# The b matrices of the next projection split behind the first softmax, and the coefficients evicted ahead of the second wide part

## The reference

```python
def cond(x, A, B, ids):
    Bx = jnp.einsum('bni,bri->bnr', x, B[ids])
    return jnp.einsum('bnr,bor->bno', Bx, A[ids])

def ffn(x, W, b, A, Bm, Wr):
    base_out = jnp.einsum('bsi,oi->bso', x, W) + b
    gates = jax.nn.softmax(jnp.einsum('bsi,ei->bse', x, Wr), axis=-1)
    lora_out = jnp.einsum('bser,eor->bseo', jnp.einsum('bsi,eri->bser', x, A), Bm)
    return base_out + jnp.einsum('bse,bseo->bso', gates * 2.0, lora_out)
```

## Time and profile before

| | before |
|---|---|
| median of three runs | 351.79 us (350.92 to 352.30) |
| the profiled execution, its own time | 353.02 us |
| its span, first to last instruction | 351.0 us |
| TensorE matmul busy | 326.0 us, 93% |
| VectorE busy | 246.0 us, 70% |
| ScalarE busy | 149.8 us, 43% |
| GpSimd busy | 89.9 us, 26% |
| mean granted TensorE clock | 0.976 of full |

### The profile page before, as it was taken

How to read it: one execution, slowest core, us unless ns; L and a number is a source line. 1 busy time by engine, 2 the same in 40 slices (tenths; PEclk the granted TensorE clock), 3 DMA queues, 4 the chain that set the end, 5 groups by cost and what they waited for, 6 DMA issues and landing times.

```text
span 351.0 us, 6577 instructions
## 1 busy us (share of the span) xinstructions
PE 326.0 (93%) x2112; PEld 304.6 (87%) x2112; DVE 246.0 (70%) x496; ACT 149.8 (43%) x317; POOL 89.9 (26%) x61
## 2 busy tenths in 40 slices
PE   6998747889999999999999999999999999999975
PEld 5777647879999899989999999999999999999864
DVE  5925993797586867697668767775878586855554
ACT  5856833663065405550456036613562166203210
POOL 0014620184015500550046003620262026300000
PEclk9999898969999999999999999999999999999989
DMA  6889526611782078405950586048803780140005
GB/s 276 327 278 326 181 92 203 219 58 51 250 269 92 17 228 287 132 2 166 302 189 0 143 289 225 0 120 268 266 5 98 245 296 18 49 190 2 0 23 218
DMA packets 31525, 56.17 MB, mean 160 GB/s; under 512 B 3793, under 2 KB 21074, under 8 KB 31506
## 3 DMA queue, kind: packets, MB, share of 16 engines
q1 hardware_dynamic: 31506, 55.94, 47.9%
HBM read 39.15 MB, written 16.78 MB: 159 GB/s over the span
## 4 chain that ended last, share of the span: by engine, by line
PE 53%; issue 12%; DMA 10%; DVE 9%; POOL 6%; SPq 5%; ACT 4%; POOLq 0%; ACTq 0%; DVEq 0%
PE ps_d L316 12%; PE ps_d L318 12%; PE ps_d L317 12%; POOL xs_lo L917 5%; DMA xraw<-w 4%; DMA out<-xraw 3%; PE ps_h L323 3%; PE ps_p L316 2%; DVE k_lo L684 2%; PE ps_p L317 2%; PE ps_p L318 2%; PE ps_t L447 2%; DMA abraw<-ab_tab 2%; SPq L233 2%; SPq L235 2%
## 5 line engine op out<-in xcount | busy, mean ns | idle before, releaser
L917 POOL TENSOR_TENSOR xs_lo<-xraw,xs_hi 128x512 fp32r<-128x512 f32 x48 | 67.8, 1423 | 195.4 <-ACT xs_hi L520 195.3
L316 PE MATMUL ps_d<-w1s_hi,a1s_hi 128*128 128x384 f32 (+1 forms) x216 | 72.7, 337 | 1.8 <-DVE w1s_lo L684 1.8
L318 PE MATMUL ps_d<-w1s_hi,a1s_lo 128*128 128x384 f32 (+1 forms) x216 | 70.2, 325 | 0.0
L317 PE MATMUL ps_d<-w1s_lo,a1s_hi 128*128 128x384 f32 (+1 forms) x216 | 70.2, 325 | 0.0
L903 DVE SCALAR_TENSOR_TENSOR xraw<-ps_d,bsum,xraw 128x512 f32<-128x512 f32 x62 | 46.3, 750 | 27.5 <-PE ps_d L318 27.5
L520 ACT ACTIVATE xs_hi<-xraw 128x512 fp32r<-128x512 f32 x64 | 38.4, 624 | 17.6 <-DMA xraw<-x_in 11.1
L316 PEld LDWEIGHTS ps_d<-w1s_hi,a1s_hi 128*128 128x128 f32 x216 | 41.1, 190 | 3.9 <-DVE w1s_lo L684 3.8
L316 PE MATMUL ps_p<-xs_hi,bst_hi 128*128 128x256 f32 x128 | 39.4, 307 | 3.4 <-POOL xs_lo L917 2.5
L317 PEld LDWEIGHTS ps_d<-w1s_lo,a1s_hi 128*128 128x128 f32 x216 | 41.1, 190 | 0.0
L318 PEld LDWEIGHTS ps_d<-w1s_hi,a1s_lo 128*128 128x128 f32 x216 | 41.0, 190 | 0.0
L317 PE MATMUL ps_p<-xs_lo,bst_hi 128*128 128x256 f32 x128 | 37.8, 295 | 0.0
(11 more groups left out here) (156 smaller groups left out, 691.8 us busy)
## 6 DMA issues: line engine op xcount, KB each, us to landing
xraw<-x_in SPq DMA_DIRECT2D x32, 512.0 KB, 5.0
out<-xraw SPq DMA_DIRECT2D x32, 512.0 KB, 3.6
xraw<-w SPq DMA_DIRECT2D x16, 512.0 KB, 6.5
abraw<-ab_tab SPq DMA_DIRECT2D x64, 128.0 KB, 2.1
b0raw<-b_tab SPq DMA_DIRECT2D x64, 64.0 KB, 1.9
b0raw<-a SPq DMA_DIRECT2D x1, 512.0 KB, 3.7
lp<-exp SPq DMA_DIRECT2D x4, 69.0 KB, 7.5
cm<-exp_in SPq DMA_DIRECT2D x1, 144.0 KB, 5.3
```

What stands on the lines that cost most here:

```text
L316: pe.matmul(acc, lh, rh, start=first, stop=False, skip_group_check=True)
L317: pe.matmul(acc, lh, rl, start=False, stop=False, skip_group_check=True)
L318: return pe.matmul(acc, ll, rh, start=False, stop=final, skip_group_check=True)
L917: return pool.tensor_tensor(dst, whole, high.bitcast(F32), ALU.subtract)
```

## The change

On ScalarE and VectorE, in steps 1 to 6, `split_b(g + 1)` moves from the head of the step to behind the first softmax, and `coef_high(0)` / `coef_low(0)` move ahead of `wide_high(1)` / `wide_low(1)`. Step 7 has no `split_b`; there only the coefficients change places with the wide part. Step 0 keeps its order. On TensorE the wait for `f1_lo` stands ahead of `start_results` in step 7, and where it was in the others.

```diff
@@ TensorE
                 if last:
+                    pe.wait_ge(f1_lo, 2 * g + 2)
                     start_results((0, 1, 3))
                 else:
                     project(g + 1, 0)
-                pe.wait_ge(f1_lo, 2 * g + 2)
+                    pe.wait_ge(f1_lo, 2 * g + 2)
                 route(1, k2, f1s)
@@ ScalarE
                 if not first:
                     h_and_k1(g)
-                if not last and not first:
-                    split_b(g + 1)
...
                 softmax_exp(0)
                 if first:
                     experts_high()
-                wide_high(1)
-                coef_high(0)
+                    wide_high(1)
+                    coef_high(0)
+                else:
+                    if not last:
+                        split_b(g + 1)
+                    coef_high(0)
+                    wide_high(1)
@@ VectorE
                 if not first:
                     h_to_sbuf(g)
                     k1_low(g)
-                if not last and not first:
-                    split_b(g + 1)
...
                 softmax(0)
                 if first:
                     experts_low()
-                wide_low(1)
-                coef_low(0)
+                    wide_low(1)
+                    coef_low(0)
+                else:
+                    if not last:
+                        split_b(g + 1)
+                    coef_low(0)
+                    wide_low(1)
```

## The result

The changed kernel takes 357.65 us (median of four runs, 356.15 to 359.33) against 351.60 for the kernel before: ratio 1.0163, interval 1.0106 to 1.0219. It is slower, by 6.0 us in these medians; the forecast was 355.9, the range 352.3 to 357.9.

What follows compares the result with a forecast made beforehand. TensorE was taken as the bound; five steps at 0.8 us (4.0) plus 0.1 for step 2 gave 4.1 us, on 351.8 a forecast of 355.9 us. The range meant to hold 8 in 10 was 352.3 to 357.9.

Steps and rivals of the forecast that it cites:

- The bound and the head of the step: TensorE bounds the loop; removing the b splits from the step's head, where they fill a gap, gains 0.
- ScalarE, VectorE, the coefficients: Behind the first softmax: coefficients reach TensorE 0.24 us later, costing 0.12 us, and everything that follows moves by 0.12.
- GpSimd's chunks and the reversal: Second half: GpSimd's chunks come late, GpSimd starts 0.18 us ahead of VectorE's `xs_lo`, and TensorE gets that chunk later.
- The price of a step: Steps 1, 3, 4, 5 and 6: 0.8 us each from the late chunk, 4.0 us together.
- Step 2 has its stall already: 0.1: Step 2 already had GpSimd ahead of VectorE at `xs_lo`, so the change adds only 0.1 us there.
- the forecast's own: The forecast's narrower range, 354.8 to 357.5 us, from 0.6 to 1.1 us in five steps.
- No reversal (1): VectorE stays ahead of GpSimd at `xs_lo`; a step costs 0.12 to 0.15 us, 351.8 to 352.5 us; chance 0.15.
- Rival 2: VectorE slower behind the softmax, coefficients 0.37 us late, VectorE stays first; about 2 us, 353.9 us; chance 0.08.
- Rival 4: Late `xs_lo` makes `turn()` wait too, or step 2 pays in full; 1.2 to 1.4 us a step; chance 0.07.

Runs made afterwards that it cites:

- the second measurement: The changed kernel again, unaltered, in more rounds against the kernel before: 358.58 us against 352.52, ratio 1.0149 (1.0101 to 1.0197).

## Why the prediction was right, and where its sizes were off

**The bound and the head of the step: right.** In steps 3 to 6 the exponential and `turn()` stand where they stood, to 0.01 us (step 2 is another matter, below). The b splits lay in a gap, and taking them out of it brought nothing.

**ScalarE, VectorE, the coefficients: right.** The weight load comes at 16.55 (forecast 16.53), and what follows moved by 0.14 (forecast 0.12): `ps_s` from 17.43 to 17.57. Where both kernels read `k_lo` from PSUM, the change costs 0.12 us a step, as this term alone would.

**GpSimd's chunks and the reversal: right, to 0.03 us in each line of the table.** The margin, forecast at 0.18, was 0.20. That the reversal is the larger part was tested from two sides: with the order held in both kernels 0.35 of the 0.85 remain, and with `k_lo` out of GpSimd's way in both kernels 0.12 remain. So of the 0.85 some 0.12 is the late coefficients, 0.23 that the first `k_lo<-cm` is held up longer (1.49 us, where it took 1.27), and 0.50 the reversal.

**The price of a step: 0.85 where 0.8 was said.** The same terms: the chunk reaches TensorE 0.73 later where 0.70 was said, the first matmul behind the wait costs its 0.10, and 0.02 more is added by the end of the step.

**Step 2: the term that was mis-sized.** "Step 2 has its stall already: 0.1" was wrong; it cost 0.44 (0.50 in the second execution of the changed kernel). The stall was indeed there already, but everything ahead of it moved by far more than the 0.12 of the other steps: VectorE's operation on `ps_s` went from 17.30 to 17.78 us into the step. In the kernel before, an x chunk landed late in step 2 (ScalarE waited 1.29 us for it). So GpSimd started its second chunk at 141.80, behind the softmax's subtraction on `lg` at 141.43, which took its 0.18 us; it held up only a later operation of the softmax, for less, and what follows came 0.13 us sooner than in step 4.

In this execution of the changed kernel the chunk was copied 0.5 us earlier in the step. GpSimd started at 142.16, ahead of the subtraction at 142.26, which took 1.22 us. The exponential moved from 11.19 to 12.23 us into the step, and what follows it came 0.21 later than in step 4. With the 0.14 of the other steps these two, 0.13 and 0.21, make up the 0.48. The second execution had a late chunk again, with the subtraction at 0.17 us, and its step 2 took 37.32 all the same. So the course of step 2 depends on when a chunk lands, which the prediction did not consider.

The sum is 4.7 us in the trace, not 4.1: 0.34 of the difference is step 2, the rest the five times 0.05.

**The rest, 351.6 + 4.7 = 356.3 against a median of 357.65.** Both intervals of the ratio hold 4.7 us. The median lies within the range (to 357.9) but just outside the forecast's own (to 357.5; its terms add up to 357.4). What the second measurement leaves above it (5.2) isn't explained by anything in the traces and may be the spread of single runs.

**The rivals.** No reversal (1) did not come true for the changed kernel, but did for the b splits alone, where all is 1.0 us late: there too it was no gain. Rival 2, slower operations on VectorE: the four `bst_lo` took 2.48 us (218.68 to 221.16), as worked out. The prediction says that the trace disagrees with the Trainium skill there; it doesn't, for the passage that it names (VectorE: DVE Perf Modes, The DRAIN you can't avoid) goes on that a next operation that is not held starts earlier, and the 0.60 from start to start of operations that take 0.68 agree with that. Rival 4 did not happen; `turn()` of the second layer did not wait longer.

## What to carry to other kernels

Before moving work on an engine that is not the bound, ask what the work behind it triggers on a third engine, and when. Here eight operations, hidden where they stood, were moved to where they delayed ScalarE's copies of the coefficients by 0.4 us, VectorE's low parts of them by 1.3 and GpSimd by 1.4. With the order of the two engines held, 0.35 us a step of all that reached TensorE; the larger part, 0.50, came because the delay changed which of two engines was first at a shared resource, 0.03 us apart before. Where two engines hold each other up, list the pairs of operations that run at the same time with their margins, and take the one that TensorE waits for off the shared path (here by reading one input from PSUM) before tuning the order; a wait that forces the order has a price too (0.24 us a step).

## What the runs showed of the hardware that was not expected

That GpSimd and VectorE hold each other up was in the prediction, and so were its sizes for `k_lo` and `xs_lo`. In all traces it goes by whole instructions, and whoever starts first is not held. VectorE's `k_lo` of two SBUF inputs, 0.42 us alone, took 1.27 to 1.50 beside GpSimd and ended 0.26 to 0.29 after GpSimd's end; `xs_lo`, 0.69 alone, took 1.66; GpSimd, 1.29 alone, took 1.81 when VectorE was 0.03 ahead and 1.29 when it was itself ahead. Even an operation of 16 columns (`lg`) took 1.20 us in this way, against 0.18, which the prediction did not use. The held operation ends its own time less some 0.15 us after the other's end: 0.27 for one of 0.42, 0.54 to 0.57 for one of 0.69, 0.03 for one of 0.18. Operations with one input in PSUM kept their time beside GpSimd (`k_lo<-ps_s`, 0.42 us at 222.34, while GpSimd ran until 223.00). The Trainium skill, GPSIMD Engine Reference, Key points, names the contention and the kind of instruction, and the traces agree; that a few hundredths of a microsecond decide 0.5 us a step is what these runs show.
